# An attention block in split precision: value products of two steps issued together, scores first in every other slot, and one staging slot moved from the input to the low probabilities

## What is computed

```python
x = ft.reshape(B, N, C)                       # 16, 1024, 512
qkv = x @ w_qkv + b_qkv
q, k, v = jnp.split(qkv.reshape(B, N, N_HEADS, 3 * D_HEAD), 3, axis=-1)
attn = jnp.einsum('bxhd,byhd->bxyh', q, k) * SCALE
attn = jax.nn.softmax(attn, axis=2)
res = jnp.einsum('bxyh,byhd->bxhd', attn, v).reshape(B, N, N_HEADS * D_HEAD)
return (res @ w_out + b_out + x).reshape(B, H, W, C)
```

## Time and profile before

| | |
|---|---|
| median of 3 runs | 3923.45 us |
| profiled execution, its own time | 3922.59 us |
| its span, first to last instruction | 3920.8 us |
| PE busy | 3823.5 us (98%), 39180 instructions |
| ACT busy | 3022.9 us (77%) |
| DVE busy | 2663.7 us (68%) |
| POOL busy | 1991.4 us (51%) |
| mean granted TensorE clock | 0.998 |

### The profile page before, as it was taken

How to read it: one execution, slowest core, us unless ns; L and a number is a source line. 1 busy time by engine, 2 the same in 40 slices (tenths; PEclk the granted TensorE clock), 3 DMA queues, 4 the chain that set the end, 5 groups by cost and what they waited for, 6 DMA issues and landing times.

```text
span 3920.8 us, 97172 instructions
## 1 busy us (share of the span) xinstructions
PE 3823.5 (98%) x39180; PEld 3143.7 (80%) x39180; DVE 2663.7 (68%) x4379; ACT 3022.9 (77%) x5141; POOL 1991.4 (51%) x1030
## 2 busy tenths in 40 slices
PE   6999999999999999999999999999999999999998
PEld 5878788787888878888787888878878788787886
DVE  5776666666676676666666676676766666666665
ACT  5887877878777787777877788787887877878776
POOL 2454544545445464454644546455454544545444
PEclk9999999999999999999999999999999999999999
DMA  2011111111112121121111211112111110111111
GB/s 89 20 51 48 53 47 26 55 42 55 47 26 58 36 58 44 26 66 31 55 47 26 68 28 53 47 34 65 26 53 47 43 57 23 52 47 47 47 26 52
DMA packets 100722, 178.49 MB, mean 46 GB/s; under 512 B 16192, under 2 KB 16192, under 8 KB 100288
## 3 DMA queue, kind: packets, MB, share of 16 engines
q1 hardware_dynamic: 100288, 172.29, 15.7%
HBM read 71.57 MB, written 33.55 MB: 27 GB/s over the span
## 4 chain that ended last, share of the span: by engine, by line
PE 90%; DVE 4%; ACT 3%; issue 2%; DMA 0%; POOL 0%; SPq 0%; ACTq 0%; DVEq 0%
PE psum L494 36%; PE psum L513 13%; PE psum L544 11%; PE psum L546 11%; PE psum L566 6%; PE psum L570 6%; PE psum L568 6%; DVE max_parts L730 1%; PE psum L503 1%; ACT p_hi L644 1%; ACT p_full L643 1%; PE psum L521 1%; DVE q_shift L716 1%; ACT q_hi_hi L626 1%; DVE p_lo L749 0%
## 5 line engine op out<-in xcount | busy, mean ns | idle before, releaser
L410 POOL TENSOR_TENSOR p_lo<-p_full,p_hi 128x1024 f16<-128x1024 f32 x768 | 1646.1, 2144 | 1746.4 <-ACT p_hi L644 1745.4
L643 ACT ACTIVATE p_full<-psum,prob_bias 128x512 f32<-128x512 f32 x2048 | 1427.9, 697 | 672.0 <-PE psum L546 664.8
L730 DVE TENSOR_REDUCE max_parts<-psum 128x1 f32<-128x512 f32 x2048 | 1379.8, 687 | 737.0 <-PE psum L513 729.9
L644 ACT ACTIVATE p_hi<-psum,prob_bias 128x512 f16<-128x512 f32 x2048 | 1424.1, 695 | 0.0
L566 PEld LDWEIGHTS psum<-v_parts,p_hi 128*128 128x128 f16 x8192 | 744.5, 98 | 243.6 <-issue 153.9
L513 PE MATMUL psum<-k_lo_hi,q_hi_hi 128*128 128x512 f32 x2048 | 848.0, 435 | 25.2 <-issue 22.2
L566 PE MATMUL psum<-v_parts,p_hi 128*128 128x65 f16 x8192 | 858.8, 193 | 5.3 <-ACT p_hi L644 2.7
L568 PE MATMUL psum<-v_parts,p_hi 128*128 128x64 f16 x8192 | 852.7, 192 | 0.0
L570 PE MATMUL psum<-v_parts,p_lo 128*128 128x65 f16 x8192 | 850.2, 194 | 0.0
L544 PE MATMUL psum<-q_hi_hi,k_lo_hi 128*128 128x512 f32 x2048 | 806.0, 394 | 11.8 <-ACT p_hi L644 8.1
L546 PE MATMUL psum<-q_shift,k_shift 128*128 128x512 f32 x2048 | 801.9, 392 | 0.0
(11 more groups left out here) (59 smaller groups left out, 4721.8 us busy)
## 6 DMA issues: line engine op xcount, KB each, us to landing
x_in<-in_xT SPq DMA_DIRECT2D x128, 256.0 KB, 3.0
q_hi_hi<-q_hi_hi SPq DMA_DIRECT2D x256, 128.0 KB, 2.2
k_shift<-k_lo_hi SPq DMA_DIRECT2D x256, 128.0 KB, 2.3
y_tile<-in_x SPq DMA_DIRECT2D x128, 256.0 KB, 2.7
result<-y_tile SPq DMA_DIRECT2D x128, 256.0 KB, 2.0
o_heads<-in_L_conv_w_qkv SPq DMA_DIRECT2D x12, 256.0 KB, 4.1
o_heads<-in_L_conv_w_out SPq DMA_DIRECT2D x4, 256.0 KB, 4.9
out_bias<-in_L_conv_b_out SPq DMA_DIRECT2D x1, 256.0 KB, 4.3
```

What stands on the lines that cost most here:

```text
L410: nc.gpsimd.tensor_tensor(p_lo[:, g % LO_SLOTS, :, :], p_full[:, g % 2, :, :], p_hi[:, g % HI_SLOTS, :, :], ALU.subtract).then_inc(p_lo_re ...
L643: nc.scalar.activation(p_full[:, g % 2, n, :], scores(g, n), ACT.Exp, scale=SCALE, bias=prob_bias[:, :])
L644: nc.scalar.activation(p_hi[:, g % HI_SLOTS, n, :], scores(g, n), ACT.Exp, scale=SCALE, bias=prob_bias[:, :]).then_inc(exp_done, 1)
L730: nc.vector.reduce_max(max_parts[:, u % 2, q_tile, k_half:k_half + 1], bank(b, w), AX.X).then_inc(done["row_max"], 1)
```

## The change

`LO_SLOTS` goes from 2 to 3 and `X_SLOTS` from 3 to 2. In odd slots PE issues the scores of the next step ahead of the fills and issues no value products. In even slots the scores stay behind the fills, and the value products of steps g-2 and g-1 follow together. ACT, DVE and POOL keep their order of instructions.

```diff
-X_SLOTS, Y_SLOTS, O_SLOTS, HI_SLOTS, LO_SLOTS = 3, 3, 3, 4, 2
+X_SLOTS, Y_SLOTS, O_SLOTS, HI_SLOTS, LO_SLOTS = 2, 3, 3, 4, 3
...
                     for w in transposes_of_slot(g - STEPS * b):
                         transpose(b, w)
+
+                if g % 2 == 1 and is_step(g + 1):
+                    step_scores(g + 1)
                 for b in batches:
                     for piece in fills_of_slot(g - STEPS * b):
                         fill(b, *piece)
-                if is_step(g + 1):
+                if g % 2 == 0 and is_step(g + 1):
                     step_scores(g + 1)
                 for b in batches:
                     for w in ring_late(g - STEPS * b):
                         ring(b, w)
                 if g == 0:
                     bias_through_w_out()
-                if is_step(g - 1):
+
+                if g % 2 == 0 and is_step(g - 1):
+                    step_pv(g - 2)
                     step_pv(g - 1)
```

## The result

The changed kernel takes 4042.85 us (median of 4 runs, 4040.18 to 4044.66), against 3923.06 us for the kernel before. The ratio is 1.0304, 95% interval 1.0287 to 1.0322: slower by 120 us, where 88 were forecast (4011, range 3950 to 4065).

What follows compares the result with a forecast made beforehand. PE was taken to bound the kernel, at 98% of the span. From the profiled 3922.59 us: -44 seams, +80 input slots, +45 fill banks, +3 start, +5 other waits = +89, giving 4011 us, range 3950 to 4065.

Steps and rivals of the forecast that it cites:

- Part 1: Changes from value products to other work on PE: 512 fewer at 0.086 us each, 44 us saved, bounds 40 and 50.
- Part 2: Two input slots instead of three: casts wait for loads around slots 48 to 52, 80 us lost, bounds 65 and 110.
- PE waits 1.9 us at step 50: PE's second score tile of step 50 waits 1.9 us for exponentials queued behind a late input cast.
- part 2: Piece of the next image's input, cast by ACT in slot 48; its load was to make ACT wait 2.4 us.
- part 5: Later piece of the input, its load behind two SP copies; ACT was to wait 2.4 us, delaying step 52's second score tile.
- 5.3 us an image: Delay of the scores of step 53 from both input waits, in 15 images, giving the 80 us lost.
- The clock: Rival, chance 0.12: new waits drop PE's clock once an image, 15 x 1.9 = 28 us more, 4040 us.
- Part 3: Fill banks claimed before DVE drains them, slots 3-4, 5-6, 7-8 and 61-62: 45 us lost, bounds 20 and 60.
- only the input waits: Rival, chance 0.13: DVE's drains are ready in time, the 45 us of bank waits vanish, 3966 us.
- Part 4: The rest: program start 3 us later from input loads, and about 5 us of waits in slots 34 and 42.
- the transposition at slots 34 and 42: Without fills there, transposing the row maxima waits for two reductions: 0.7 us less today's waits, about 5 us in all.

Runs made afterwards that it cites:

- e2: Changed kernel with X_SLOTS back to 3 and LO_SLOTS back to 2, so the new order on the old buffers: 3952.5 us, ratio 1.0071.
- e1: Kernel before with X_SLOTS 2 instead of 3 and nothing else: 4012.4 us, ratio 1.0225.
- e9: Changed kernel with one cast moved, part 5 of the input in slot 51 instead of 50: 3991.2 us, ratio 1.0171.
- e3: Changed kernel with the casts of the input's parts spread over slots 47 to 55 instead of 47 to 52: 4005.1 us, ratio 1.0205.
- e4: Changed kernel with DVE in odd slots draining output projections or v ahead of the late row-max tile: 3989.1 us, ratio 1.0166.
- e5: Changed kernel with the edits of e2 and e4 together: 3903.0 us, ratio 0.9946.
- e8: e6 with DVE's drains first in odd slots: 3894.4 us, ratio 0.9924.
- e6: Changed kernel with scores behind the fills in all slots, only value products in pairs, X_SLOTS 3 and LO_SLOTS 2: 3966.0 us, ratio 1.0105.
- e7: Changed kernel with only the scores ahead of fills in odd slots, value products unpaired, X_SLOTS 3 and LO_SLOTS 2: 3944.3 us, ratio 1.005.
- e10: Kernel before with DVE's drains first in odd slots and nothing else: 3905.0 us, ratio 0.9951.

## Why the prediction was right

**Part 1, seams: right, somewhat too small.** Forecast 0.086 us for each of 512, and that is what the distances show (0.315 us against 0.229 for the next). But each block of value products that no longer starts by itself saves a little more: its first three distances are 0.039, 0.034 and 0.032 us before, against 0.029 later in the block; in pairs they are 0.034, 0.033 and 0.033. Together that is 0.11 us for two steps. Quiet stretches are 0.09 to 0.16 us faster with one seam less, 0.12 in the mean. That is 56 to 61 us for 512, over the bound of 50.

**Part 2, the input: right in mechanism; right in size only because the clock made up for a wait that was not there.** Forecast 80 us without the clock; e2 against the changed kernel gives 90 with it. By the starts of the scores 88 us of it lie behind the program's start; the clock's falls are 31 of them, so the waits themselves cost 57 and not 80. The step "PE waits 1.9 us at step 50" failed. PE's second score tile of that step starts 0.50 us behind the first on average, against 0.46 before: 0.04 us of wait. ACT did wait for part 2, 1.25 us on average and not 2.4. DVE's and POOL's subtractions of slot 47 overlap, and the one that starts later takes longer (last section). Here POOL's first one, which frees the slot, was spared: it took 1.28 us instead of 2.06, so the load went out earlier. And PE came later itself, held by a row-max bank (L513 on `max_parts`, 11.7 us).

At part 5 ACT waited 3.2 us on average, where I had 2.4. The load landed 3.6 us after its issue in the median, up to 4.9, where I took the 3.0 of all loads. It has two copies ahead of it and a load of y behind it in the queue; that these slow it is likely but not tested. PE's idle time at step 52 was 3.8 us, against the 4.4 that I counted without its own delays and the 3.4 that my 5.3 us an image leave beside the 1.9 at step 50.

**The clock: a rival at 0.12 that came true beside the forecast.** 15 falls of 1.3 to 2.7 us, 2.1 in the mean, are 31 us. I had priced them at 28 and left them out of the sum. With them the rival's sum is 4040, 3 us from the measured time; but that closeness is luck too, since it holds the 80 us of part 2. As the Trainium skill has it ("TensorE: Matmul & The Clock Gate", "Why this matters for your kernels"), gaps over about 3 us between bursts are to be avoided. The changed kernel agrees, with a fall behind 3.0 to 5.0 us of idle PE in every one of fifteen images. Shorter gaps are not safe, though: nine of e1's eleven falls, both of e9's and all four of e3's (behind the first image's start) came behind 1.7 to 2.6 us at the longest, and there the measurement decides. The kernel before has one too, which the prediction overlooked: behind 2.3 us of idle PE at 3883.4 us its clock is 0.50 from 3886.8 us on.

**Part 3, fill banks: right.** Forecast 1.72 us from tile to free bank, measured 1.72; 0.77 us of wait, measured 0.71 in the record. Forecast 45 us. The five stretches stand 56 us above quiet ones; draining first gives 49.5 us back in e4 (there alone) and in e5 against e2. The working went through slots 4, 6, 8 and 62 and missed slot 64 (step 1 in the table, +0.42), where PE's wait for `v_parts` rose from 0.73 to 1.27 us an image. The rival "only the input waits" falls.

**Part 4: the start right, the rest right in sign and too small.** The first scores of step 1 come 4.4 us later than before (forecast 3), in e1 2.3 and in e2 0.4, so this is the input's slot. Outside the fill banks' five stretches, e2 holds 34 us more than quiet stretches would, 1.8 us an image of it at steps 43 to 53, where I had 0.3. e8 shows part of it without the rest: +0.74, +0.83 and +0.30 at steps 47, 51 and 55. What I had named, the transposition at slots 34 and 42, is there (PE L521 on `row_max`, 0.54 us each time instead of 0.15), but the larger pieces lie elsewhere. The last section takes up the largest.

**The sum,** from the starts of all scores: 511 stretches at the quiet 0.119 us give -61 us (forecast -44). Fill banks are +56 (45), the input's waits +57 (80), the clock +31 (nothing), other waits +34 (5), and the program's start +4 (3). That makes 121, and the last score products lie 121.5 us later than before. So the input's waits were 23 us too large and the gain of the seams 17 too small, against 31 us of clock, 29 of other waits and 11 of fill banks that were missing. Errors of both signs met: the direction and the main mechanisms were right, the closeness of 4011 to 4043 is partly luck.

## What to carry to other kernels

When a reorder is paid for with a buffer, price the buffer's loss by itself: here one staging slot of 2 KB a partition cost 88 to 90 us, more than the 44 (forecast) to 61 us (quiet stretches) that the reorder saves, and the slot that it bought was hardly used. Between the end of a product group and the next claim of its bank, count what the draining engine does first: moving one drain ahead of one reduction was worth 19 us in the kernel before and 50 to 72 us in the reordered ones. Put a control beside the best version: most of its gain came from the repair and not from the idea.

## What the runs showed of the hardware

A float32 weight load (0.19 us) behind 65-column products that start 0.03 us apart costs 0.086 us of array time: in 985 of the 1023 changes of the kernel before, the second start behind it comes after 0.29 to 0.34 us, median 0.315, against 0.229 for the next.

Falls of the granted clock to 0.50 came behind idle times of PE as short as 1.7 us, and a fall cost 1.3 to 2.7 us in the changed kernel. Idle times of up to 2.5 us in e9 passed without one, so their length alone doesn't decide.

Where two subtractions of float32 into the low part overlap, one on DVE and one on POOL, the later one pays. In slot 47 of the kernel before, DVE starts at 2153.63 and takes 1.23 us; POOL starts at 2153.93, and its two take 2.06 and 1.29. In the changed kernel it is POOL at 2218.18 and DVE at 2218.30; POOL's two take 1.29 and 2.26:

```profile
2218.18 3.50 POOL L404 TENSOR_TENSOR xT_lo<-x_in,xT_hi 128x512 fp32r<-128x512 f32 x2 [3.87 <-ACT xT_hi L605]
```
```profile
2218.30 2.25 DVE L754 TENSOR_TENSOR p_lo<-p_full,p_hi 128x1024 f16<-128x1024 f32 x1
2220.48 1.96 DVE L735 TENSOR_REDUCE max_parts<-psum 128x1 f32<-128x512 f32 x3
```

Each stretched one ends 1.1 us after the other's end, nearly what it takes alone. With DVE's start 0.12 us behind POOL's its 1.23 us become 2.25, and three row maxima queue behind it. It is this way in slot 47 of images 0 to 14 in all eight kernels with value products in pairs (the changed one, e2 to e6, e8, e9), and the other way round in the four without (before, e1, e7, e10).

PE waits 0.63 us for `max_parts` in slot 48 of image 8, but the collision is not what makes it wait. The last image has no next input to cast and subtract; there DVE's subtraction takes 1.23 us, and PE still waits 0.54 us for that bank. The stretch to step 51 stands at +0.43 there in the changed kernel, against +1.00 in the mean of images 0 to 14 (e8: +0.41 against +0.87). So about half of this piece comes with the pairs alone, and the other half with the input's work in these slots, of which the collision is a part that no run tells apart.
